# One attention and mixture-of-experts block on one core: four heads at once in 32-row tiles of TensorE, and each score bank's mask pieces directly behind its products

## What is computed

```python
Q, K, V = x @ W_q + b_q, x @ W_k + b_k, x @ W_v + b_v        # of the layernormed x, 16 heads of 8
scores = (Q K^T + Q . rel_k[clip(k - q, -2, 2) + 2]) / sqrt(8)
attn = softmax(where(k <= q, scores, -1e9))
out = (attn V + attn . rel_v[...]) @ W_o + b_o
x = x + layernorm(out)
x = x + layernorm(silu(h sw1) * (h sw3) sw2 + sum of the two best experts' gelu(h ew1) ew2)   # h = layernorm(x)
```

## Time and profile before

| what | value |
|---|---|
| three runs | 1034.72, 1034.78, 1037.62 us (median 1034.78) |
| profiled execution, first to last instruction | 1036.5 us |
| DVE busy | 833.7 us (80%) |
| PE busy | 896.3 us (86%) |
| ACT, POOL busy | 676.3 us (65%), 727.1 us (70%) |

### The profile page before, as it was taken

One profiled execution on the slowest core, in us unless ns is written; L12 is line 12 of the kernel. 1 busy time (PEld: TensorE's weight loads), 2 busy tenths in 40 slices (PEclk: granted clock), 3 DMA queues, 4 the chain that ended last, 5 costly groups with the idle time before them and its releaser, 6 DMA issues. The chain is left out here.

```text
span 1036.5 us, 23477 instructions
## 1 busy us (share of the span) xinstructions
PE 896.3 (86%) x7655; PEld 513.6 (50%) x7655; DVE 833.7 (80%) x1948; ACT 676.3 (65%) x1305; POOL 727.1 (70%) x940
## 2 busy tenths in 40 slices
PE   2778889889889898898898988986679999999995
PEld 0324444444444444444444444432457777777773
DVE  5578888888988888889888888877568788878884
ACT  2038677777676777776777777765447767676773
POOL 4135686876867868768678687576357989898886
PEclk9769999999999999999999999988889999999999
DMA  2610110110101101011011011101425455555441
GB/s 48 170 44 34 35 44 31 47 42 32 49 31 42 45 32 47 32 43 49 32 42 44 33 47 40 35 18 50 148 59 169 144 165 150 169 151 166 162 140 31
DMA packets 64004, 74.93 MB, mean 72 GB/s; under 512 B 10032, under 2 KB 39600, under 8 KB 63904
## 3 DMA queue, kind: packets, MB, share of 16 engines
q1 hardware_dynamic: 61536, 73.17, 22.4%
q10 hardware_dynamic: 2368, 0.48, 0.3%
HBM read 43.75 MB, written 8.65 MB: 51 GB/s over the span
## 5 line engine op out<-in xcount | busy, mean ns | idle before, releaser
L1128 DVE TENSOR_REDUCE mx<-ps_s 128x1 f32<-128x512 f32 (+2 forms) x640 | 408.6, 681 | 84.3 <-PE ps_s L1540 83.7
L799 ACT ACTIVATE prob<-ps_e 128x512 f32<-128x512 f32 x640 | 349.6, 606 | 103.3 <-PE ps_e L1497 103.2
L641 POOL TENSOR_SCALAR_AFFINE_SELECT prob<-prob 128x516 f32<-128x516 f32 (+1 forms) x320 | 174.9, 571 | 141.8 <-ACT prob L799 141.8
L1519 PE MATMUL ps_s<-ks,qs 63*128 63x512 f16 (+3 forms) x1024 | 224.5, 312 | 47.4 <-DVE mx L1128 31.5
L1497 PE MATMUL ps_e<-qs,ks 64*128 64x512 f16 (+3 forms) x1024 | 212.1, 307 | 3.7 <-ACT prob L799 1.7
L721 POOL TENSOR_TENSOR hidden_low<-hidden,hidden_high 128x512 fp32r<-128x512 f32 x144 | 191.1, 1356 | 12.1 <-ACT hidden_high L989 10.9
L1557 PE MATMUL ps_av<-prob,vp 128*32 128x512 f32 (+3 forms) x2048 | 182.4, 452 | 4.3 <-POOL prob L641 4.2
L1519 PEld LDWEIGHTS ps_s<-ks,qs 63*128 63x128 f16 x1024 | 67.6, 95 | 184.0 <-DVE mx L1128 80.5
L989 ACT CAST hidden_high<-hidden 128x512 fp32r<-128x512 f32 x160 | 98.0, 612 | 30.5 <-DVE hidden L1441 27.3
L1540 PE MATMUL ps_s<-masked_at,below_r 64*128 64x128 bf16 (+3 forms) x640 | 103.1, 211 | 0.0
L1540 PE MATMUL ps_s<-masked_at,below 64*128 64x128 bf16 (+3 forms) x640 | 91.3, 213 | 0.0
(11 more groups left out here) (177 smaller groups left out, 1737.7 us busy)
## 6 DMA issues: line engine op xcount, KB each, us to landing
gate_rows<-gates_dram SPq DMA_DIRECT2D x128, 256.0 KB, 3.6
qs<-qh SPq DMA_DIRECT2D x128, 32.0 KB
qs<-ql SPq DMA_DIRECT2D x128, 32.0 KB
xnT_dram<-oT SPq DMA_DIRECT2D x16, 256.0 KB, 2.0
xeT<-xnT_dram SPq DMA_DIRECT2D x16, 256.0 KB, 2.7
out<-result SPq DMA_DIRECT2D x16, 256.0 KB, 2.3
v_near<-v_back SPq DMA_DIRECT2D x16, 254.0 KB
ks<-kh SPq DMA_DIRECT2D x124, 32.0 KB
```

Source lines behind the costliest of these rows:

```text
L641: pool.affine_select(out=v, in_=v, compare_op=ALU.is_ge, fill=0.0, base=-2, pattern=cols, channel_multiplier=-1).then_inc(S["p_masked"], 1)
L799: act.activation(prob[g % 2][:, u, b, :], ps_e[bank][:, :], ACT.Exp, scale=SCALE).then_inc(S["e_done"], 1)
L1128: dve.tensor_reduce(out, src, AX.X, ALU.max).then_inc(s_free[bank], 1)
L1519: pe.matmul(scores[:, at:at + P * (qt + 1)], qs[par][rows, 2 * g + off, P * qt:P * qt + P], ks[par][rows, 2 * g + off, 0:P * (qt + 1)], st ...
```

## The change

The stacks are laid out in quarters: each head has 32 rows (three blocks of 8 rows, interleaved as rows r, r+4, ..., and row 31 for the maximum; the low x low block is left out of the sum), and there are four slots of 512 columns in place of eight. Groups with even g lie in quarters 0 and 1, those with odd g in quarters 2 and 3. The scores take the groups in the order 1, 0, 3, 2 while the exponents take 0, 1, 2, 3, so in every round the score products and the exponent products lie in different quarters: four heads, four quarters. The two copies of the triangle become four (`below[0..3]`), made by twelve copies on ACT, now behind `first_keys` and no longer at ACT's start. Half a stack takes six DMAs of 64 KB in place of sixteen of 32 KB, the first K stack three on ACT in place of eight. The mask has four pieces of 32 columns (33 for the last) for each bank in place of two of 64, and all four stand directly behind that bank's products. POOL makes eight small selects for `masked_at` in place of four and four for `m_col` in place of two; DVE's fills of the stacks are half as long. `masked_columns`, the weight order and the constants follow the new layout.

```diff
@@ heads laid in quarters of the rows @@
+def quad(g, b):
+    return slice(QUAD * (2 * (g % 2) + b), QUAD * (2 * (g % 2) + b) + QUAD)
+def slot(g, off):
+    return 2 * (g // 2) + off
+S_GROUP = [1, 0, 3, 2]
-HALF = P // 2
-M_ROW = HALF - 1
+QUAD = P // 4
+M_ROW = QUAD - 1
-            qs0 = sb_attention("qs0", [P, NPAIR, SEQ], F16)
+            qs0 = sb_attention("qs0", [P, NSLOT, SEQ], F16)
...
@@ SP: stacks_out @@
-                for stk, parts in ((qs[par], (qh, qh, ql, ql)), (ks[par], (kh, kl, kh, kl))):
+                for stk, parts in ((qs[par], (qh, qh, ql)), (ks[par], (kh, kl, kh))):
                     if s == 0 and half == 0 and stk is ks[par]:
                         continue
-                    for b in range(2):
-                        for r, part in enumerate(parts):
-                            lo = 64 * b + D * r
-                            src = 64 * b + 32 * half
-                            sp.dma_start(stk[lo:lo + D, prs, :], part[src:src + 32, :]).then_inc(stacks[par][half], 16)
+                    for r, part in enumerate(parts):
+                        sp.dma_start(stk[r:P:4, slots, :], part[rows, :]).then_inc(stacks[par][half], 16)
...
@@ ACT: first_keys, and the turned copies of the triangle @@
-                for b in range(2):
-                    for r, part in enumerate((kh, kl, kh, kl)):
-                        lo = HALF * b + D * r
-                        act.dma_start(ks0[lo:lo + D, 0:NPAIR // 2, :],
-                                      part[HALF * b:HALF * b + 32, :]).then_inc(stacks[0][0], 16)
+                for r, part in enumerate((kh, kl, kh)):
+                    act.dma_start(ks0[r:P:4, 0:NSLOT // 2, :], part[0:64, :]).then_inc(stacks[0][0], 16)
-            def roll_halves():
+            def roll_quads():
                 act.wait_ge(S["const_ready"], N_POOL_CONST)
-                act.copy(below_r[0:HALF, :], below[HALF:P, :]).then_inc(S["rolled"], 1)
-                act.copy(below_r[HALF:P, :], below[0:HALF, :]).then_inc(S["rolled"], 1)
+                for turn in range(1, 4):
+                    for c in range(4):
+                        src = QUAD * ((c + turn) % 4)
+                        act.copy(below[turn][QUAD * c:QUAD * c + QUAD, :],
+                                 below[0][src:src + QUAD, :]).then_inc(S["rolled"], 1)
-            roll_halves()
...
                 if st.t0 == 0:
                     first_keys()
+                    roll_quads()
...
@@ PE: products and masks @@
-                par, rows = st.a % 2, slice(HALF * b, HALF * b + M_ROW)
+                first_row = quad(S_GROUP[g], b).start
+                par, rows = st.a % 2, slice(first_row, first_row + M_ROW)
...
-            def s_masks(u, both):
-                n = len(S_UNITS[u])
-                for part in range(2):
-                    for b in (1, 0):
-                        rows = slice(HALF * b, HALF * b + HALF)
-                        columns = masked_at[rows, 0:HALF + part].unsqueeze(1).to_broadcast([HALF, n, HALF + part])
-                        last = pe.matmul(diagonals(both[b], u, part), (below if b == part else below_r)[rows, :],
-                                         columns, start=False, stop=(part == 1))
+            def s_mask(g, u, bank, part, b):
+                n, rows = len(S_UNITS[u]), quad(g, b)
+                width = QUAD + (part == 3)
+                columns = masked_at[rows, 0:width].unsqueeze(1).to_broadcast([QUAD, n, width])
+                last = pe.matmul(diagonals(bank, u, part), below[(part - rows.start // QUAD) % 4][rows, :],
+                                 columns, start=False, stop=(part == 3))
+                if part == 3:
+                    last.then_inc(S["s_full"], 1)
+            def s_masks(g, u, bank, b):
+                for part in range(4):
+                    s_mask(g, u, bank, part, b)
...
                         if st.B:
                             e_part(st, 2 * r, exps, n)
+                    if st.A:
+                        s_masks(S_GROUP[g], u, both[1], 1)
                     if st.B:
                         exps = e_unit(st, 2 * r + 1)
...
                     if st.A:
-                        s_masks(u, both)
+                        s_masks(S_GROUP[g], u, both[0], 0)
```

More of the change, by code:

```diff
@@ L20 @@
 NPAIR, NGRP = H // 2, H // 4
+NSLOT = H // 4
 SCALE = float(D) ** -0.5
@@ L236, in block_kernel @@
         ident16 = sb("ident16", [P, P], F16)
-        below = sb("below", [P, P], BF16)
-        below_r = sb("below_r", [P, P], BF16)
-        masked_at = sb("masked_at", [P, HALF + 1], BF16)
+        below = [sb(f"below{i}", [P, P], BF16) for i in range(4)]
+        masked_at = sb("masked_at", [P, QUAD + 1], BF16)
         head_sel = sb("head_sel", [P, D, NPAIR, 2])
@@ L441, in stacks_out @@
             def stacks_out(st, s, half):
-                par, prs = s % 2, slice(4 * half, 4 * half + 4)
+                par, slots, rows = s % 2, slice(2 * half, 2 * half + 2), slice(64 * half, 64 * half + 64)
                 if s < 2:
@@ L581, in _ @@
                                    pattern=[[-1, P]], channel_multiplier=1).then_inc(S["const_ready"], 1)
-            pool.affine_select(out=below[:, :], in_=below[:, :], compare_op=ALU.is_ge, fill=0.0, base=0,
+            pool.affine_select(out=below[0][:, :], in_=below[0][:, :], compare_op=ALU.is_ge, fill=0.0, base=0,
                                pattern=[[-1, P]], channel_multiplier=1).then_inc(S["const_ready"], 1)
-            for half in range(2):
-                v = head_sel[:, :, 4 * half:4 * half + 4, :]
-                pool.affine_select(out=v, in_=v, compare_op=ALU.not_equal, fill=1.0, base=-32 * half,
-                                   pattern=[[-4, D], [-1, NPAIR // 2], [-64, 2]],
+            for off in range(2):
+                v = head_sel[:, :, off:NPAIR:2, :]
+                pool.affine_select(out=v, in_=v, compare_op=ALU.not_equal, fill=1.0, base=-off,
+                                   pattern=[[-2, D], [-32, NPAIR // 2], [-16, 2]],
```

71 lines of the change are left out of this document (36 added, 35 removed).

## The result

| | before | changed |
|---|---|---|
| median of the runs | 1036.2 us (4 runs, 1034.7 to 1037.8) | 1070.8 us (4 runs, 1067.1 to 1076.3) |
| changed / before | | 1.032, 95% interval 1.030 to 1.035 |
| profiled span | 1036.5 us | 1072.7 us |
| mean granted TensorE clock | 0.960 | 0.904 |
| DVE's first score maximum | 31.6 us | 26.95 us |

The forecast was 1026 us with a range of 1015 to 1038, and a chance of 0.13 for slower. The kernel became slower by 34.6 us, outside the range. What lies behind the last score maximum, the last exponents and the experts' part, stayed as it was (347.5 us before, 346.7 us after). The profiled loss up to there is 37.0 us, although the start had gained 9.4 us. One execution of b_early (1107.1 us) and one of b64_fill (2316.9 us) were in a slow state and are left out of all figures here.

The account below looks back on a forecast made before the run. DVE's work was taken to bound full steps, so only its waits and the start could change the time: -2.0 us for full steps and -7.0 for the start, off the median 1034.8, gave 1026 us, range 1015 to 1038.

Parts of the forecast that it names:

- at a TensorE clock of 0.99: Full steps, 153 to 690 us, kernel before: DVE busy 87% with TensorE at the 2.4 GHz level.
- the term of the full steps: Thirteen full steps: shorter DVE waits against longer PE rounds, -0.15 us a step, -2.0 us in all.
- The rival "slower": Rounds 6 to 9: mask pieces in one quarter don't hide weight loads; up to +20 us, 1055 us; chance 0.13.
- my s of 0.027: Distance between two mask pieces in one quarter, taken as 0.027 us; 0.098 us if weight loads are not hidden.
- near 30s - 0.9: Change of a full step in us with the mask-piece distance s left open; slower by 0.3% from s = 0.056.
- Unit 6's gain: DVE's wait at unit 6 of a full step: 0.17 us gained, since PE's round before waited for DVE itself.
- the rival "the full steps gain more": Waits swallow PE's loss in rounds 6 to 9: 0.54 us gained a step, -14.0 in all, 1021 us; chance 0.18.
- DVE's work stays as it is in full steps: Full steps: DVE's 35.8 us of work a step stays fixed, so only waits and the start change the time.
- PE's round: First bank full 0.30 us in; second exponent and score products start then; round 0.05 to 0.11 us longer.
- The start: Pipeline start, steps 1 to 3: fewer DMAs and earlier masks against twelve late copies, -7.0 us, bounded by 0 and -9.5.
- the first step's waits: Step 1, low clock: DVE's waits of about 0.2 us in many rounds; six go with early masks, -1.2 us.
- my 28.9: Step 1: DVE's first maximum at 28.9 us and not at 31.56, -2.6 us.

Follow-up runs that it names:

- b_early: The kernel before (64-row halves), with only the first bank's two mask pieces moved directly behind that bank's products, ahead of the second pair; 1036.5 us, ratio 0.999.
- b64_fill: b64_early_dma with seven overwritten repeats of exponent products on 64 rows, in rounds 13, 15 and 16 of a step; 1013.9 us, ratio 0.978.
- a_fill128: The changed kernel with ten extra overwritten products a step, reading all 128 rows, in rounds where PE waited; 1031.4 us, ratio 0.994.
- a_rows64: The changed kernel, same order and DMAs, with score, exponent and mask products reading 64 rows (63 for scores); output not the reference's; 1029.3 us, ratio 0.993.
- a_fill: The changed kernel with ten repeated, overwritten exponent products of one quarter a step, in rounds where PE waited; 1050.4 us, ratio 1.015.
- a_late: The changed kernel with all eight mask pieces at the end of the round, alternating between the two banks; 1032.3 us, ratio 0.995.
- a_four: The changed kernel with the first bank's four mask pieces behind all four products, ahead of the second bank's four; 1021.9 us, ratio 0.985.
- b64_early_dma: b_early with the changed kernel's larger transfers (six DMAs for half a stack) and the low x low block left out; 1017.5 us, ratio 0.981.
- a_e64: The changed kernel with only the exponent products on 64 rows, scores and masks staying in 32; output not the reference's; 1672.3 us, ratio 1.614.
- a_four_fill_b: a_four with ten extra overwritten 128-row products a step and five more in rounds 17, 18 and 0; 1026.1 us, ratio 0.988.

## Why the prediction was wrong

**The step that failed** is the first: "at a TensorE clock of 0.99". That was read from the kernel before and carried over to the changed one, and no rival asked what the new products would do to it. In the sum it is the term of the full steps, -0.15 us a step or -2.0 us, which came out at +3.0 us a step or +39.1 us, at a clock of 0.88. At 2.4 GHz a step in the changed order takes 40.8 us (a_fill128) or, with 64 rows, 41.5 us (a_rows64); the thirteen full steps took 575.7 us (150.3 to 726.0), which is 45 or 36 us more. Against the kernel before the account is: -9.4 us up to step 2's first maximum, +7.3 us in steps 2 and 3 (88.3 for 81.0 us), and +39.1 us in the thirteen full steps (575.7 for 536.6): +37.0 us.

**The cause** of the lost time is the low clock: a_rows64, a_fill and a_fill128 keep the order of the changed kernel's queue, and each gets time back with the clock. What makes the clock fall is less sure. The best reading of these runs is two things that come together, products of 32 rows and longer pauses of PE; they are not fully separated. From the traces, one full step each (pauses over 0.5 us by the ends of PE's products; falls as the granted clock has them):

| kernel | rows | PE's pauses, us | falls to 1.2 GHz |
|---|---|---|---|
| before | 64 | 0.90, 0.70, 0.68, 0.75 | 3.4 us past 38 us in 2 of 12, none in the others |
| b_early | 64 | 1.34, 1.38 (and 0.75 without a fall) | 3.4 to 6.8 us in half the steps |
| a_rows64 | 64 | 1.10, 0.67, 0.64, 0.61 | none |
| changed | 32 | 1.26, 1.35 | 3.4 and 6.8 us in every step from 7 to 15 |
| a_late | 32 | 1.51, 1.37 | 3.4 or 6.8 us past 30 us in 9 of 12; behind the first pause in 2 of 12 |
| a_four | 32 | 1.37, 1.39 | 3.4 or 6.8 us past 30 us in 8 of 12; behind the first pause in none |
| a_fill | 32 | 0.69, 0.57 | 6.8 us in most |
| a_fill128 | 32, repeats 128 | 0.71 | 6.8 us in some |

b_early against the changed kernel has nearly the same pauses and other rows: none to 6.8 us of low clock a step for 10.2. It also has half as many mask pieces; its transfers are others too, but b64_early_dma, with the changed kernel's, has the same pauses (1.32, 1.38) as b_early and like falls, of 3.4 or 6.8 us in 7 of 12 steps. a_fill against a_fill128 has the same columns in the same rounds and other rows, 19 us, but shorter pauses as well. Pauses matter too: b_early against before, where only masks have moved, and a_fill against the changed kernel, 20 us. And the order matters: a_four has the rows of the changed kernel, and its first pause, at the same place, is longer (1.37 for 1.26), yet no fall follows it. There four products start at once, where the changed kernel starts two; whether it is the number of rows at work at a time that counts no run here has tested.

The Trainium skill puts falls of the clock down to waits of the engine (TensorE: Matmul & The Clock Gate, HAM oscillation — how this bites in real kernels). These runs agree in so far as longer pauses brought falls (b_early for before). They add that rows or order bear on it too, since b_early, a_four and the changed kernel differ at like pauses, and in a_e64 the clock fell with no pause over 0.5 us.

**The rival "slower"** had the right sign from the wrong place: its mechanism, weight loads that nothing hides, did not occur. Pieces in one quarter stand 0.025 to 0.034 us apart, for my s of 0.027. The Trainium skill's rule that I weighed there, a weight load beside products in flight only when the row group differs (TensorE: Matmul & The Clock Gate, Part 3, The mechanism), is not borne out by this trace: the four pieces of a bank are in one row group, and one of their loads lasts 100 ns. The rival's sum, near 30s - 0.9, leaves out some of the terms that its text names; with all of them it is nearer 39s - 1.2, which at s = 0.028 is still about nought and changes nothing here.

**Full steps at a held clock.** Forecast -0.15 us a step. Unit 6's gain came as forecast (0.18 for 0.17). As a whole the step gains 0.7 us in b_early (40.7 for 41.4) and 0.6 in a_fill128 (40.8, though with repeats in it), near the 0.54 of the rival "the full steps gain more", but by luck: the waits ahead of maxima did not shrink (4.5 us in b_early, 4.7 in a_fill128, for 4.4). The gain is DVE's busy time, 36.0 us a step before and 34.5 and 34.6 in these two, which the prediction had held fixed ("DVE's work stays as it is in full steps"). In a_rows64, with eight pieces of 64 rows, a step gains nothing (41.5). And in 32 rows the early masks cost time: with the masks at the end (a_late) or behind all four products (a_four) a step takes 40.1 us. That they would keep four quarters from running at once the prediction had said; it did not price it.

**PE's round.** I had the second exponent and score products start at 0.30 us, behind all four pieces. In the row above the exponent product starts at 403.73, 0.24 into the round and behind the first piece only, and so does the score product where no bank is missing (384.59 in the round from 384.35). In the row above it waited for its bank until 0.45. The first bank is full when I said (0.31 us into the round).

**The start.** Forecast -5.3 us by step 2 and -1.2 in the first step's waits, measured -9.4 by step 2's first maximum, at the edge of my -9.5. The first maximum stands 2 us before my 28.9: the third of the K stack's DMAs was issued at 20.46 and not at 22.1 (the first was issued at 19.17 and not at 20.08, and they are 0.65 us apart, where I had taken the first at 1.33), so the copies ran from 21.12 and PE's bias product was released at 25.03. The copies' own price was right.

**Open.** Steps 3 to 5 took 46.7 to 47.9 us, with 20, 21 and 16 us at 1.2 GHz; I did not find out why these and not the later ones. Nor did I separate what the number of pieces, eight for four in a round, adds to the falls, nor rows, rows at work at a time and pauses from one another. Why a small DVE operation lasts until POOL's ends is not shown either, only that it does.

## What to carry to other kernels

Where a change makes TensorE's products smaller in rows or regroups them, the granted clock of the kernel before is no longer given: price one step at 1.2 GHz as a rival, and look at PEclk first in the profile after. Four small row tiles side by side saved at most 1.3 us of a 41.4 us step here (a_late, a_four), and falls of the clock took back all of it in a_late and 0.8 us in a_four; in the changed kernel, which starts two at a time, they took 3.6 us (44.4 for 40.8). The same transfers and the same early masks in 64-row halves gave 1.9%, and the transfers alone 1.2%. Where the clock falls behind a wait of PE, a few products whose result is overwritten can be cheaper than the fall, as long as they do not stand ahead of what another engine waits for. And a step can change without any of its waits: look whether the busy time of the engine that decides is still the same.

## What the runs showed that I had not expected

- Work that nobody needs made a kernel faster: ten 128-row products a step took the changed kernel from 1070.8 to 1031.4 us.
- Products of 31 and of 64 rows in turn start one by one, 0.15 to 0.27 us apart, and not in pairs; with the clock that came with it (0.59) the kernel took 1.6 times as long (a_e64).
- A small operation of DVE that starts just behind one of POOL took 1.03 us and ended with it; started just ahead of it, it took 0.19 us (the kernel before, b_early).
- A lower mean clock need not be slower: a_four at 0.917 takes 1021.9 us, a_four_fill_b at 0.971 takes 1026.1. Their full steps take the same 40.9 us in the mean, at 0.94 and 0.99.
